# Rank-one attention of the last layer: keys on partitions, arguments and weighted sums as tiled TensorE products, averages taken in the stage before

## The reference, cut to what matters

```python
x_avg = jnp.mean(x, axis=(2, 3), keepdims=True)
se_mid = relu(conv1x1(x_avg, se1_w, se1_b))
W_cw = sigmoid(conv1x1(se_mid, se2_w, se2_b))       # one gate per image and channel
g_x = conv1x1(x, g_w, g_b).reshape(b, N)            # N = 1024 pixels
theta_x = conv1x1(x, theta_w, theta_b).reshape(b, N)
phi_x = conv1x1(x, phi_w, phi_b).reshape(b, N)
f = theta_x[:, :, None] * phi_x[:, None, :]         # 1024 x 1024 per image
y = einsum('bij,bj->bi', softmax(f, axis=-1), g_x)
W_y = conv1x1(y, W_w, W_b)
W_y = (W_y - bn_mean) * (bn_gamma / sqrt(bn_var + eps)) + bn_beta
return W_cw * W_y + x
```

## Time and profile before

| | us |
|---|---|
| median of 3 runs | 2871.19 (2867.9 to 2873.26) |
| profiled execution, its own time | 2870.26 |
| its span, first to last instruction | 2868.5 |
| begin of the last stage (first instruction after the barrier) | 2802.30 |

### The profile page before, as it was taken

How to read it: one execution, slowest core, us unless ns; L and a number is a source line. 1 busy time by engine, 2 the same in 40 slices (tenths; PEclk the granted TensorE clock), 3 DMA queues, 4 the chain that set the end, 5 groups by cost and what they waited for, 6 DMA issues and landing times. The chain is left out here.

```text
span 2868.5 us, 45618 instructions
## 1 busy us (share of the span) xinstructions
PE 2717.4 (95%) x19977; PEld 1355.9 (47%) x19977; DVE 2182.4 (76%) x1415; ACT 1672.2 (58%) x2588; POOL 100.4 (3%) x65
## 2 busy tenths in 40 slices
PE   7399999999999999999999999999799999999893
PEld 3334444444444444334444344344578888757551
DVE  5499999999999999999999999998542221234447
ACT  2467776777777767777677777766522222211335
POOL 0000000000000000000000000000440000000004
PEclk9699999999999999999999999999899999999996
DMA  1100000000000000000000000000600000200001
GB/s 69 41 23 22 23 29 9 29 29 16 29 13 32 29 9 29 22 23 29 9 29 29 16 29 18 27 5 1 195 1 0 1 1 2 82 0 1 0 1 59
DMA packets 37607, 72.24 MB, mean 25 GB/s; under 512 B 20960, under 2 KB 21920, under 8 KB 35744
## 3 DMA queue, kind: packets, MB, share of 16 engines
q1 hardware_dynamic: 37344, 69.19, 7.2%
q0 software_dynamic: 64, 0.13, 0.0%
HBM read 60.45 MB, written 8.86 MB: 24 GB/s over the span
## 5 line engine op out<-in xcount | busy, mean ns | idle before, releaser
L734 PE MATMUL l_ps<-mlp_w,W2H 128*64 128x512 f16 x8192 | 1366.5, 392 | 17.2 <-DVE mlp_w L768 17.2
L768 DVE TENSOR_TENSOR mlp_w<-words_x,words_y 128x2048 f32<-128x2048 f32 x512 | 1159.5, 2287 | 66.9 <-PE l_ps L734 66.9
L734 PE MATMUL l_ps<-mlp_w,W2L 128*64 128x512 f16 x4096 | 802.3, 388 | 0.0
L734 PEld LDWEIGHTS l_ps<-mlp_w,W2H 128*64 128x64 f16 x8192 | 455.2, 108 | 549.3 <-issue 116.4
L815 ACT ACTIVATE relu_bottom<-l_ps 128x512 f32<-128x512 f32 x1024 | 612.3, 598 | 79.5 <-PE l_ps L734 1.4
L815 ACT ACTIVATE mlp_w<-l_ps 128x512 f32<-128x512 f32 x684 | 408.8, 598 | 279.7 <-PE l_ps L734 249.7
L752 DVE SCALAR_TENSOR_TENSOR mlp_w<-relu_bottom,sign_ratio,mlp_w 128x2048 f32<-128x2048 f32 x171 | 401.4, 2347 | 7.6 <-ACT relu_bottom L815 7.6
L734 PEld LDWEIGHTS l_ps<-mlp_w,W2L 128*64 128x64 f16 x4096 | 229.0, 109 | 179.7 <-issue 0.8
L815 ACT ACTIVATE relu_top<-l_ps 128x512 f32<-128x512 f32 x340 | 203.2, 598 | 135.7 <-PE l_ps L734 120.8
L723 PE MATMUL l_ps<-y_rows,y_weights_halves 12*128 12x512 bf16 x2048 | 202.4, 385 | 12.1 <-DMA y_rows<-y_pieces 12.1
L752 DVE SCALAR_TENSOR_TENSOR relu_top<-relu_bottom,sign_ratio,relu_top 128x2048 f32<-128x2048 f32 x85 | 199.6, 2349 | 4.0 <-ACT relu_bottom L815 4.0
(11 more groups left out here) (343 smaller groups left out, 2578.8 us busy)
## 6 DMA issues: line engine op xcount, KB each, us to landing
table_pos<-pos_table SPq DMA_DIRECT2D x64, 512.0 KB, 3.6
mlp_w<-in_mlp_w SPq DMA_DIRECT2D x8, 1024.0 KB, 14.0
X<-in_x SPq DMA_DIRECT2D x8, 512.0 KB, 7.6
bias_scratch<-bias_rows SPq DMA_DIRECT2D x64, 64.0 KB, 2.0
mlp_w_hi<-bias_scratch SPq DMA_DIRECT2D x16, 256.0 KB, 3.8
out<-Q SPq DMA_DIRECT2D x8, 512.0 KB, 2.7
y_rows<-y_pieces SPq DMA_DIRECT2D x192, 12.0 KB
xn_b<-in_out_wT SPq DMA_DIRECT2D x1, 1024.0 KB, 6.9
```

Of the source, the lines that this page charges most:

```text
L734: last = nc.tensor.matmul(out[q][a * DH:(a + 1) * DH, :], w[:, half], h[a][:, :, k], start=False, stop=stop, tile_position=(0, a * DH))
L768: nc.vector.tensor_tensor(hw[i % 3][:, r].rearrange("p (m j) -> p m j", j=J), words_x, words_y[:, 2 * n + r].unsqueeze(1).to_broadcast([P, ...
```

## The change

In the last stage the keys lie on partitions and the queries along the row:
- Two selecting matrices made by GpSimd (`sel_q`, `sel_k`) turn `rows` into operands with two useful rows in each group of 32 partitions. The row pair on the query side holds the query and minus its bound, the pair on the key side the key and a one (the bias of row 3 of each group, from the new constant `rank`). So one product with two rows gives query x key minus bound for 128 keys x 512 queries. A round `arguments(r)` is four such products, at partitions 0, 32, 64 and 96, two for each of two tiles of PSUM (128 x 1024); the second pair has a wait of its own.
- ScalarE takes only the exponential of a tile, 16 tiles in all (L1857), from PSUM, with no sum, scale or bias.
- `weigh(r)` sums over the keys as a product: the turned rows (values and a row of ones among them, `rows_t`) as 32-column weights, the exponentials as the moving operand, four products side by side in four column positions; eight rounds, four per image, accumulate in PSUM.
- The four partial results are turned (`columns`), added and divided on eight columns (`quotient`), and spread by four products per half image (`replicate`), straight from the quotient column and the identity. VectorE makes all sixteen output tiles of 128 x 512 (`outputs`); the stores are sixteen of 256 KB.
- The gate is 1 / (1 + exp(-x)), and the square root of the variance moves to the stage before. VectorE adds the shift to X for both images (L1807), GpSimd no longer does.
- The averages are taken by ScalarE in the stage before: the first image's while it waits for TensorE's sums, the second's on half tiles, each after VectorE's addition (L1604 in the new file).

```diff
                 if k in TAIL:
                     b = TAIL[k]
                     for t in range(NT):
-                        act.wait_ge(z_mm, b * NT + t + 1)
                         if b:
                             act.wait_ge(o_mm, b * NT * CC)
+                            for c in range(2 * t, 2 * t + 2):
+                                act.wait_ge(o_out, NT * CC)
+                                nc.scalar.activation(ex[c % 2], K.X[:, c, 0], ACT.Copy, accum_out=K.av[:, c, 0:1]).then_inc(mean, 1)
+                                act.wait_ge(mean, c + 1)
+                        act.wait_ge(z_mm, b * NT + t + 1)
                         nc.scalar.activation(z[:, t * BANK:(t + 1) * BANK], zps[t][:], ACT.Copy).then_inc(z_out, 1)
+            for i in range(NT * CC):
+                t, c = divmod(i, CC)
+                act.wait_ge(o_out, (B - 1) * NT * CC + i + 1)
+                act.wait_ge(mean, CC + i)
+                nc.scalar.activation(ex[2][:, 0:BANK], K.X[:, c, B - 1, t * BANK:(t + 1) * BANK], ACT.Copy,
+                                     accum_out=(K.av_b[:, c:c + 1] if t else K.av[:, c, 1:2])).then_inc(mean, 1)
...
+            pe.wait_ge(sel, 3 + 4 * B * NT)
+            nc.tensor.matmul(args[0][:, 0], sel_q[:, 0], rows, start=True, stop=True).then_inc(qk_mm, 1)
+            nc.tensor.matmul(args[0][:, 1], sel_k[:, 0], rows, start=True, stop=True).then_inc(qk_mm, 1)
...
+            def arguments(r):
+                b, jj = divmod(r, JJ)
+                pe.wait_ge(q_out, b + 1)
+                pe.wait_ge(k_out, b + 1)
+                for t in range(NT):
+                    k = NT * r + t
+                    if k == 1:
+                        pe.wait_ge(ends, 4)
+                    if k == 2:
+                        pe.wait_ge(t_out, 1)
+                        pe.wait_ge(k_out, 2)
+                    if k >= 3:
+                        pe.wait_ge(ex, k - 2)
+                    for u in range(2):
+                        at = 32 * (2 * t + u)
+                        last = nc.tensor.matmul(args[k % 3][:, u], keys[b][at:at + 2, jj * P:(jj + 1) * P], queries[b][at:at + 2, :],
+                                                start=True, stop=True, tile_position=(at, 0))
+                    last.then_inc(a_mm, 1)
+
+            def weigh(r):
+                b, jj = divmod(r, JJ)
+                if r == 0:
+                    pe.wait_ge(q_out, 2)
+                    pe.wait_ge(t_out, 1)
+                if jj == 0 and b:
+                    pe.wait_ge(gx, 1)
+                pe.wait_ge(ex, NT * (r + 1))
+                for t in range(NT):
+                    k = NT * r + t
+                    for u in range(2):
+                        at, n = 32 * (2 * t + u), 32 * (NT * b + u)
+                        last = nc.tensor.matmul(acc[b][at:at + 32, :], rows_t[:, jj, n:n + 32], e[k % EB][:, u],
+                                                start=(jj == 0), stop=(jj == JJ - 1), tile_position=(0, at))
+                last.then_inc(s_mm, 1)
...
+            def replicate(b, t):
+                pe.wait_ge(col, 4 * (b + 1))
+                if b == 0 and t:
+                    pe.wait_ge(o_out, CC)
+                for r in range(JJ):
+                    last = nc.tensor.matmul(y_ps(b, t)[:, r * P:(r + 1) * P], num[:, b, r, t:t + 1].to_broadcast([P, P]), K.k("ident"),
+                                            start=True, stop=True)
+                last.then_inc(y_mm, 1)
+
+            for r in range(B * JJ):
+                arguments(r)
+                if r:
+                    weigh(r - 1)
+                if r == JJ + 1:
+                    columns(0)
+                if r == JJ + 2:
+                    replicate(0, 0)
+            weigh(B * JJ - 1)
+            replicate(0, 1)
+            columns(1)
+            for t in range(NT):
+                replicate(1, t)
 
         @block.vector
...
+            dve.wait_ge(gx, 1)
+            nc.vector.tensor_scalar(gate[:], gate[:], 1.0, None, ALU.add).then_inc(coef, 1)
+            dve.wait_ge(coef, 1)
+            nc.vector.reciprocal(gate[:], gate[:]).then_inc(coef, 1)
+            dve.wait_ge(coef, 2)
+            nc.vector.tensor_tensor(ga[:], gate[:], K.bn_a[:].unsqueeze(2).to_broadcast([P, CC, B]), ALU.mult).then_inc(coef, 1)
+            nc.vector.tensor_tensor(gd[:], gate[:], K.bn_t[:].unsqueeze(2).to_broadcast([P, CC, B]), ALU.mult).then_inc(coef, 1)
+            dve.wait_ge(coef, 4)
+            for b in range(B):
+                for c in range(CC):
+                    nc.vector.tensor_scalar(K.X[:, c, b], K.X[:, c, b], gd[:, c, b:b + 1], None, ALU.add).then_inc(xg, 1)
+
...
+                nc.vector.tensor_tensor(num[:, b], num[:, b], den[:, b], ALU.mult).then_inc(col, 1)
+
+            def outputs(b, t):
+                dve.wait_ge(y_mm, NT * b + t + 1)
+                dve.wait_ge(xg, CC * (b + 1))
+                part = slice(t * BANK, (t + 1) * BANK)
+                for c in range(CC):
+                    nc.vector.scalar_tensor_tensor(out[:, CC * b + c, part], y_ps(b, t), ga[:, c, b:b + 1], K.X[:, c, b, part],
+                                                   ALU.mult, ALU.add).then_inc(o_out, 1)
+
+            dve.wait_ge(s_mm, JJ)
+            nc.vector.tensor_copy(sums[0], gps[:]).then_inc(s_out, 1)
+            quotient(0)
+            outputs(0, 0)
+            outputs(0, 1)
+            quotient(1)
+            outputs(1, 0)
+            outputs(1, 1)
 
...
+            for k in range(TILES):
+                act.wait_ge(a_mm, k + 1)
+                if k >= EB:
+                    act.wait_ge(s_mm, (k - EB) // NT + 1)
+                nc.scalar.activation(e[k % EB], args[k % 3][:], ACT.Exp).then_inc(ex, 1)
+            act.wait_ge(s_mm, B * JJ)
```

More of the change, by code:

```diff
@@ L1590, in stage_rank_one @@
     d = K.dram
-    se1, se2 = K.se1, K.se2
+    se1, se2, av = K.se1, K.se2, K.av
     room = carver(K.WR)
[L1593 to L1597, removed]
-    gw = sb("gtp_w32", [P, CC, 32])
-    sel = sb("row_select", [P, 2, B * NT, P])
-    th = sb("theta", [P, B * PC])
-    av, mid, gate = sb("avg", [P, CC, B]), sb("se_mid", [SE, B]), sb("gate", [P, CC, B])
@@ L1610, in stage_rank_one @@
[L1610 to L1622, removed]
+    EB, JJ = 6, BANK // P
+    TILES = 2 * B * JJ
+    e = [room([P, 2, BANK]) for _ in range(EB)]
@@ new lines, in stage_rank_one @@
+    rows, rows_t = room([P, BANK]), room([P, JJ, P])
+    queries, keys = [room([P, BANK]) for _ in range(B)], [room([P, BANK]) for _ in range(B)]
+    scaled = [room([P, BANK]) for _ in range(B)]
+    sums = [room([P, BANK]) for _ in range(B)]
+    sel_q, sel_k, sel_m = room([P, B, P]), room([P, B, P]), room([P, B * NT, P])
+    out = carver(K.Q)([P, CC * B, HW])
+    gw = sb("gtp_w32", [P, CC, 32])
+    mid, gate = sb("se_mid", [SE, B]), sb("gate", [P, CC, B])
+    ga, gd = sb("ga", [P, CC, B]), sb("gd", [P, CC, B])
@@ new lines, in stage_rank_one @@
+    rb, nb = sb("row_bias", [P, 1]), sb("se2_neg", [P, CC])
+    mm, mx = sb("phi_ends", [P, 2]), sb("phi_ext", [P, B, 2])
+    num, den = sb("r1_num", [P, B, JJ, NT]), sb("r1_den", [P, B, JJ, NT])
+    gps, small = ps("gtp_ps", [P, BANK]), ps("small_ps", [P, BANK])
+    aps, mps = small[:, 0:BLK].rearrange("p (c b) -> p c b", b=B), small[0:SE, P:P + B]
+    args = [ps(f"arg_ps{i}", [P, 2, BANK]) for i in range(3)]
+    pps = args[1][:, 0, 0:2 * B * NT]
+    sel, w_pad, head = K.sem("selection"), K.sem("gtp_w_padded"), K.sem("r1_small")
@@ L1677, in _ @@
             last.then_inc(se, 1)
-            pe.wait_ge(ones_done, 1)
-            for n in range(B * PC):
-                b, s = divmod(n, PC)
-                pe.wait_ge(ydg, n + 1)
-                nc.tensor.matmul(yps[:, b, s * P:(s + 1) * P], ones[:], dg[n % PC], start=True, stop=True).then_inc(y_mm, 1)
+            def arguments(r):
[16 more added lines that the diff above has]
+                    last.then_inc(a_mm, 1)
@@ new lines, in columns @@
+            def columns(b):
+                pe.wait_ge(s_out, b + 1)
+                for r in range(JJ):
+                    last = nc.tensor.transpose(turned[b][:, r * P:(r + 1) * P], sums[b][:, r * P:(r + 1) * P], K.k("ident"))
+                last.then_inc(c_mm, 1)
+            def replicate(b, t):
+                pe.wait_ge(col, 4 * (b + 1))
+                if b == 0 and t:
+                    pe.wait_ge(o_out, CC)
+                for r in range(JJ):
+                    last = nc.tensor.matmul(y_ps(b, t)[:, r * P:(r + 1) * P], num[:, b, r, t:t + 1].to_broadcast([P, P]), K.k("ident"),
+                                            start=True, stop=True)
+                last.then_inc(y_mm, 1)
@@ L1747, in _ @@
[L1747 to L1758 removed]
+            dve.wait_ge(g_out, 1)
@@ L1760, in _ @@
+            quotient(0)
[4 more added lines that the diff above has]
+            outputs(1, 1)
         @block.scalar
         def _(act):
```

(8 more changed lines are left out.)

220 lines of the change are left out of this document (97 added, 123 removed).

## The result

| | us | ratio to before, 95% interval |
|---|---|---|
| before, runs beside those of the change | 2868.82 (2866.39 to 2873.26) | |
| with the change | 2864.64 (2860.53 to 2867.85) | 0.9983 [0.9976, 0.9991] |
| forecast | 2853 (2845 to 2863) | |

The change makes the kernel faster, by 4 to 5 us of 2869: 4.2 between the medians, 4.9 by the ratio, 2.6 to 6.9 by its interval. The forecast was 17.5 us less, and the time lies above the range. The profiled execution took 2865.91, its span is 2864.1 us.

A forecast was written before the change was run, and what follows sets the result against it. Bound: the last stage's 66.2 us chain through one engine at a time, VectorE's weighted sums deciding its loop. New stage 0.8 + 46.9 + 1.0 = 48.7 us, 17.5 less: 2870.26 to 2852.8, predicted 2853 us (2845 to 2863).

The forecast's parts named there:

- The averages: Averages moved ahead of the last stage: stage begins 0.8 us later, `rows` is there at 4.9 us instead of 6.3.
- The operands: Last stage from `rows` to the first exponential: selection hidden, first exponential 12.1 us after the barrier, against 20.3.
- The products side by side: Loop: four two-row products take 1.3 us, half overlapping; with weighing and changes 2.3 us a round, TensorE setting the pace.
- rival (A): Loop: all four two-row products run side by side and the clock stays high; 2848 us, chance 0.22.
- a drain: Loop: changing tiling mode drains TensorE, 0.19 us a change instead of 0.11; loop 1.4 us longer, 2854 us.
- The loop's clock: TensorE at full clock in the loop; 1.0 us allowed in all for idle times before first products and last spreadings.
- (C): TensorE stays at 1.2 GHz through the loop, rounds of 4.4 us, 18 us more: 2871, or 2878; chance 0.07.
- The end: After the last exponential: last weighing, spreadings, twelve VectorE outputs and last store, about 15 us, ending at 46.9.
- The sum: Whole last stage: 0.8 + 46.9 + 1.0 = 48.7 us where 66.2 were, 17.5 us less.

The follow-up runs named there:

- the 32-row kernel: Argument products take all 32 rows of their group (30 of them zeros) instead of two, against the changed kernel; 2850.43 us, 0.9931 of before.

## Why the prediction was wrong

**The averages.** The 0.8 us in front of the barrier came out: the stage begins at 2804.22, 1.9 later than before, of which 1.1 is the whole trace running later (the third layer's product before it, 2778.67 against 2777.51). `rows` is there at 5.0 us (4.9 foreseen). That they give 0.6 us net (1.4 for 0.8) was wrong by 0.8 us: they cost 0.2, by one trace each. The table load lay in the same stretch, and I credited its going to them.

**The operands.** Right: first exponential at 12.0 (12.1). GpSimd's tiny copies took 0.18 us each, with the last wide one done at 2807.49, hidden. The steps between came as added up: the transposes done at 8.3 us (8.3 foreseen), the last two wide products at 10.0 (10.1). The front is 8.3 us shorter; of these, 1.6 are the half clock in the trace of before.

**The products side by side.** Step mis-sized, without harm: I took 1.3 us for four two-row products, half overlapping, and 0.11 for a change. In the 32-row kernel, at 2.4 GHz, the next weighing starts 1.07 and 1.24 us after them in turns, so both pairs lie side by side, as in rival (A). A weighing was 0.99 (0.88 and a change of 0.11, as foreseen). But the round of 2.15 is 0.39 longer than twice 0.88, 0.2 for each of its two changes if all of it is theirs; that is nearer to the 0.19 that the prediction works out for a drain than to its 0.11, and no run takes the changes apart from the rest. With the clock up the loop is 18.6, where I had 19.7.

**The loop's clock.** This is the step that failed: "I allow 1.0 us in all", with (C) at 0.07. The granted clock was 0.50 for 27.3 us. The sum was 10.8 us short in the loop, to the last exponential's end at 42.6 instead of 31.8. I had priced (C) at 18 us; it cost 11.9 in the loop and its start (the 32-row kernel tells), 1.6 at the end, 13.5 in all. It cost less than priced since a round went from 2.15 to 3.89 us, 1.7 more and not 2.1, and since the clock was up for the first arguments and for the last. My argument against it was that TensorE's list is full and that the earlier trace rows show full clock at 87% busy. Both are true, and neither settled it: that stretch was full-row products, and in the loop a busy share of 100% went with half clock. The prediction itself named two-row products as light work, the right ground, and gave it too little weight. The Trainium skill, TensorE: Matmul & The Clock Gate, What's actually happening, on which I leaned beside it, speaks of how busy the engine has been; as a share of time that does not suffice by the traces, since 8.00 of 8.00 us busy went with 0.50 at two and twelve rows and 1.00 at 24 and 32.

**The end.** 17.3 us, 2.2 more than the sum: the last weighing 1.73 for 1.07, the first spreading 2.0 for 1.0, the second 2.1 for 1.3, all at half clock, which makes 2.5; the rest was 0.3 shorter. With 32 rows it was 15.7, the second spreading still at half clock after 2.98 us of idle time. Sixteen small stores were no cost: the last output ends at 2861.48 and the span 2.6 us later (2.7 foreseen).

**The sum.** The prediction adds 0.9 us to 2852.8 for the median and writes 2853; its own sum gives 2853.7. That changes nothing here.

**Where the gain went.** By the table the change wins 8.3 us in front, 2.8 in the loop, and loses 4.8 at the end: 6.3 of the stage's 66.2, less 0.8 in front of the barrier. VectorE's 28.8 us of sums, 9.6 of them contention, went as foreseen, but TensorE at 1.2 GHz took their place. That makes 5.5 us; the runs say 4.2 (medians) or 4.9 (ratio). Of the 8.3, 1.6 are an accident of the traced execution of before, whose clock was down in front.

**What stays open.** Why 24 rows hold the clock and 12 don't, and whether it is the rows of the argument products alone or their mixture with the other products of a round; no kernel was run with the weighing or the arguments alone. That the other products count is likely, since the clock came back with two-row and twelve-row arguments too, 2.0 and 1.1 us after the 128-row spreading of the first image began. The zeros went into both operands, weights and moving, and which of them matters was not tried either. Open is also why the clock fell in front of the loop in one trace of the old code and not in another.

## What to carry to other kernels

Products that use few of TensorE's 128 rows (here four side by side, with two rows each) can cost the clock of everything around them, though the engine's list is full: when a change brings such products into a loop, try them with the rows filled up with zeros, which cost nothing here and gave 13.5 us in the traces. Before crediting a removed operation, look for what else went in the same stretch (here the table load stood behind the averages), and before crediting a new algorithm, take the contention away from the old one: 9 of the 33 us of its loop were GpSimd's.

## What the runs showed of the hardware

- Granted clock in a loop of argument products and full-row weighings with TensorE busy 8.00 of 8.00 us: 0.50 with arguments of 2 and 12 rows (four side by side), 1.00 with 24 and 32, though all rows but two hold zeros. It came back, without a pause in the work, 1.1 us after the first 32-row product.
- Four 32-bit products in four row positions run side by side: 1.07 to 1.24 us for the four at 2.4 GHz with the change between row and column positions, 2.0 at 1.2 GHz; two wide 32-bit products one after the other start 0.86 us apart.
- VectorE's weighted sums of 128x1024 took 3.28 us beside GpSimd's adding of two 128x1024 tiles, 1.14 to 1.23 (six) and 1.97 to 2.05 us (two) beside its shifting of such tiles, and 1.22 without GpSimd.
